# Four of a pass's sixteen GpSimd products by C moved to VectorE in a Mamba scan

## The reference

```
delta = softplus(xc @ xd_w @ dtp_w + dtp_b)
Bm, Cm = xc @ xB_w, xc @ xC_w
dA  = exp(delta[..., None] * A)                    # 512 channels x 16 states
dBx = (delta * xc)[..., None] * Bm[:, :, None, :]
h_t = dA_t * h_(t-1) + dBx_t                       # for each channel and state
y_t = sum over the 16 states of h_t * C_t;  y = y + D * xc
out = y * silu(z) @ out_w + res
```

## Time and profile before

| | us |
|---|---|
| median of 3 runs (lowest, highest) | 10204.22 (10203.43, 10209.12) |
| the profiled execution | 10211.62 |
| its span on the core | 10209.9 |

### The profile page before, as it was taken

How to read it: one execution, slowest core, us unless ns; L and a number is a source line. 1 busy time by engine, 2 the same in 40 slices (tenths; PEclk the granted TensorE clock), 3 DMA queues, 4 the chain that set the end, 5 groups by cost and what they waited for, 6 DMA issues and landing times. The chain is left out here.

```text
span 10209.9 us, 153036 instructions
## 1 busy us (share of the span) xinstructions
PE 8288.9 (81%) x42776; PEld 6783.2 (66%) x42776; DVE 8054.5 (79%) x10482; ACT 5907.1 (58%) x9202; POOL 7026.4 (69%) x7227
## 2 busy tenths in 40 slices
PE   5787878787878787878787878787878776999998
PEld 4666666666666666666666666666666664777776
DVE  4989898989898989898989898989898993333332
ACT  4656566666665666666666666666666662544443
POOL 4878788888888888888888888888888882000000
PEclk8888888888988888889898888888988887999998
DMA  2222222222222222222222222222222220000000
GB/s 92 99 90 94 100 94 98 95 99 94 97 97 91 94 96 96 98 96 94 89 89 86 94 94 100 94 99 93 100 94 100 94 84 24 11 12 8 12 10 9
DMA packets 414834, 818.78 MB, mean 80 GB/s; under 512 B 148918, under 2 KB 194138, under 8 KB 414042
## 3 DMA queue, kind: packets, MB, share of 16 engines
q1 hardware_dynamic: 410328, 806.69, 23.3%
q10 hardware_dynamic: 3714, 2.89, 0.1%
HBM read 783.16 MB, written 26.30 MB: 79 GB/s over the span
## 5 line engine op out<-in xcount | busy, mean ns | idle before, releaser
L781 ACT ACTIVATE decay<-delta,neg_a 128x512 f32<-128x512 f32 x4096 | 2799.4, 689 | 2378.0 <-DVE h_ps L982 1145.6
L543 POOL TENSOR_TENSOR bu<-b_all,u_buf 128x512 f32<-128x512 f32 x3072 | 3573.3, 1189 | 188.8 <-DVE h_ps L982 186.2
L982 DVE TENSOR_TENSOR_SCAN h_ps<-decay,bu 128x512 f32<-128x512 f32 x2304 | 2778.6, 1222 | 513.3 <-ACT decay L781 431.7
L1239 PE MATMUL y_ps<-ident,ch 128*128 128x128 f32 x16384 | 2504.0, 302 | 535.6 <-DVE ch L1002 412.8
L1239 PEld LDWEIGHTS y_ps<-ident,ch 128*128 128x128 f32 x16384 | 2132.8, 156 | 904.7 <-DVE ch L1002 552.4
L555 POOL TENSOR_TENSOR ch<-ch,c_all 128x512 f32<-128x512 f32 x1024 | 1326.3, 1295 | 966.9 <-DVE ch L982 779.1
L1002 DVE TENSOR_TENSOR ch<-h_ps,c_all 128x512 f32<-128x512 f32 x3072 | 1976.9, 671 | 0.0
L546 POOL TENSOR_TENSOR bu<-b_all,u_buf 128x514 f32<-128x514 f32 x1024 | 1244.8, 1236 | 12.7 <-DVE h_ps L982 9.1
L1123 PE MATMUL w_ps<-xn,in_w 128*128 128x257 f32 x4096 | 1095.1, 412 | 167.9 <-ACT xn L670 67.5
L986 DVE TENSOR_TENSOR_SCAN h_ps<-decay,bu 128x256 f32<-128x256 f32 x1536 | 1047.1, 737 | 59.2 <-POOL bu L546 33.9
L1123 PEld LDWEIGHTS w_ps<-xn,in_w 128*128 128x128 f32 x4096 | 806.9, 208 | 335.3 <-issue 75.7
(11 more groups left out here) (262 smaller groups left out, 11512.5 us busy)
## 6 DMA issues: line engine op xcount, KB each, us to landing
b_all<-bc_dram SPq DMA_DIRECT2D x512, 514.0 KB, 6.4
c_all<-bc_dram SPq DMA_DIRECT2D x512, 514.0 KB, 7.4
in_w<-in_L_attn_in_w SPq DMA_DIRECT2D x64, 1024.0 KB, 5.0
diag_store<-diag_dram SPq DMA_DIRECT2D x256, 256.0 KB, 3.7
x_in<-in_x SPq DMA_DIRECT2D x128, 256.0 KB, 3.6
out_w<-in_L_attn_out_w SPq DMA_DIRECT2D x64, 512.0 KB, 3.9
skip_diag<-skip_dram SPq DMA_DIRECT2D x64, 256.0 KB, 4.4
h_mid<-h_cur SPq DMA_DIRECT2D x32, 257.0 KB, 2.2
```

Source lines behind the costliest of these rows:

```text
L543: pool.tensor_tensor(bu[:, s % NBU, 0:NB * L].rearrange("p (b t) -> p b t", b=NB), b_all[:, n // NU, n % NU, :, 1:], u_buf[:, c % 2, :, 1: ...
L781: func(decay[:, s % NDP, :].rearrange("p (b t) -> p b t", b=NB), delta[:, c, :, 1:S], ACT.Exp, scale=neg_a[:, k, c, n:n + 1]).then_inc(dec ...
L982: dve.tensor_tensor_scan(h, decay[:, s % NDP, :], bu[:, s % NBU, 0:NB * L], 0.0, ALU.mult, ALU.add).then_inc(scan_done, 1)
L1239: last = pe.matmul(y_ps[:, k, :], ch[:, s % NPR, k * P:(k + 1) * P], ident[:, :], is_transpose=True, start=False, stop=(n == NST - 1 and k ...
```

## The change

`POOL_C` loses the states with n = 13 (s = 13, 29, 45, 61): GpSimd multiplies 12 states of a pass by C, VectorE 52 instead of 48. For the four states the scan writes into a PSUM slot in place of `ch`, VectorE's product follows that of state n = 12, and the counts that everyone waits for (`DVE_C`, `len(POOL_C)`) follow the list.

```diff
-POOL_C = range(1, STATES, 4)
+POOL_C = tuple(s for s in range(STATES) if s % 4 == 1 and s % NST != 13)
 DVE_C = STATES - len(POOL_C)
```

## The result

The change makes the kernel slower by 1%: 10306.29 us (median; 10297.58 to 10309.52) against 10206.67 us for the kernel before on the same chip, a ratio of 1.0098 [1.0086, 1.011], or +100 us where +49 was forecast. The direction and the engine were right, the size was not: the result lies above the range of 10215 to 10300 us. It is near the rival "Nothing hides" (10313 us) in size and shares half of its mechanism; the other half, waits for GpSimd's joint that come back, did not happen, so the nearness of the numbers is in part luck.

What follows compares the result with a forecast made beforehand. VectorE, 90% busy in the Mamba phase, was taken to set the pace. States 13, 29, 45 and 61 summed as 38 + 3 + 14 - 6 = +49 us, giving a median of 10253 us (+0.48%), range 10215 to 10300 us.

Steps and rivals of the forecast that it cites:

- Nothing hides: Rival, slower: TensorE's stretch after state 29 moves with VectorE, GpSimd joint waits come back; +109 us, 10313 us, chance 0.10.
- Who pays: VectorE sets the pace and pays 0.60 us per moved state, 154 us over 64 passes if nothing hides.
- GpSimd paces: Rival, faster: VectorE's stalls are due to GpSimd, so its relief of 5.2 us a pass gives -48 us; chance 0.04.
- Pinned SiLU: Rival: ScalarE's chain to the stall at scan 22 is not tied to scan 18, hiding state 13; +11 us, chance 0.10.
- State 13, +38: Before scan 22: ScalarE's chain moves with scan 18, so the stall keeps its length; 0.60 us every pass, 38 us.
- State 29, +3: Before `output` at scan 38: VectorE's wait for TensorE's gapless stretch hides the added 0.60 us; 3 us, bounds 0 and 38.
- thin place: Within state 29's cover: `y_t` comes about 0.6 us before TensorE wants it; charged 0.05 us, 3 us in all.
- State 45, +14: Scans 47 to 50: GpSimd's joint waits cover part, but decay 49 comes late; mean 0.22 us, 14 us.
- State 61, -6: At `step_size`: without GpSimd's product beside it, it saves 0.73 us against 0.60 us of cost; -6 us.
- Everything else at no cost: PSUM slots, counters, `ch` buffer waits, SyncE's reload and TensorE's earlier transposes were taken to cost nothing.

Runs made afterwards that it cites:

- the pair of edits: ScalarE's copies `xs_pad` and `y_t` both placed earlier: changed kernel +60.1 us against the kernel before (1.006); kernel before with both -11.3 us (0.9993).
- the fillers: Eight unused TensorE matmuls added before the projections: changed kernel +75.9 us against the kernel before (1.0074); kernel with only state 45 moved 10198.68 us (0.9998).

## Why the prediction was right or wrong, point by point

- **Who pays.** Right. VectorE pays for each added product, GpSimd's relief is worth next to nothing, and VectorE's busy time rose by 103 us (104 forecast). The rivals "GpSimd paces" and "Pinned SiLU" did not come true.
- **State 13, +38.** Paid, as forecast: +2.63 us a turn in the changed kernel, 42 us. That the sum comes so near is in part luck: it is 0.40 us in kinds 1 and 2 and 0.87 and 0.93 in kinds 3 and 4. "There is no GpSimd wait in between" was wrong: a short one before scan 16 hides 0.18 us in kinds 1 and 2, and the stall at 22 there is 1.42 instead of 1.62 us. Why kinds 3 and 4 pay more than 0.60 is not shown.
- **State 29, +3.** Wrong, and the largest miss on a single step. The step that failed is the overlap: the prediction took TensorE's stretch for its own work because its rows, of one turn, had no gap. The stretch is tied twice to VectorE's scans through ScalarE's queue. The prediction named one of the ties, `y_t` with 0.6 us of room, as the "thin place" and priced it at 3 us; in 34 of 45 passes there was no room, the stall at 38 stayed at 1.89 us, and the price is about 29 us, by the pair of edits. Of the rival "Nothing hides" this half was true.
- **State 45, +14.** The step itself was right, +0.90 us a turn (14 us): the joint's waits at 47 and 48 went, and decay 49 became late. The missing term is behind it. The prediction had TensorE's transposes start earlier "in front of nothing that VectorE waits for", at no cost; what came of it is TensorE's projections at the lower clock and the stall at `output`, 24 us by the fillers in the changed kernel, 42 in the kernel of state 45 alone. Both numbers include what fillers give in the kernel before, up to 8 us.
- **State 61, -6.** Right: the line's longest duration fell from 1410 to 695 ns, and the kernel with 61 alone is at -8.9 us.
- **Everything else at no cost.** Besides the clock, short pauses in VectorE's queue, at most 12 us.

The durations of `step_size`'s line (lowest/median/highest ns) after, against 659/684/1410 in the earlier trace rows:

```profile
L962 DVE SCALAR_TENSOR_TENSOR sp_l<-sp_l,diag_store x128: 659/674/695, 139.0 to 8477.4; 128x514 f32<-128x514 f32 x128
```

Together: 49 forecast, +26 for state 29, +16 to +24 for the clock (without or with what fillers give in the kernel before), and 0 to +12 for the pauses make 91 to 111 against 100. Each of the three is a difference of medians with an interval of some 10 us on either side, so the sum is closed no better than that. What stays open: what the pauses are, why an edit moves stalls in stretches that it doesn't touch, and why TensorE's clock falls with 45 alone by more than with all four.

## What to carry to other kernels

Before you call a stall a cover, follow its end back through every queue in order, a third engine's too: a copy that is ready may stand behind an operation that waits for the very engine whose delay you want to hide. Read more than one turn: a room of 0.6 us in one can be absent in most others. A merged row without a gap can still be slow by the clock, so look at the granted clock over just this row. And ask of a moved operation whether it shifts TensorE's work apart ahead of a dense stretch; the granted clock there belongs in the sum.

## What the runs showed of the hardware

- Work moved between two other engines changed TensorE's granted clock: the lower level went from 1.1 to 4.4 us a pass in one stretch of 10 us, and the same row of 16 records from 5.37 to 6.33 us; eight matmuls without use ahead of them gave a granted clock of 1.00, 3.68 us, and 42 us in all.
- VectorE paused for 0.37 us at places where nothing was late, and 4 or 12 fulfilled waits added to its queue removed one or both of the two pauses of a pass.
- A `scalar_tensor_tensor` with two SBUF inputs took 1.39 us beside GpSimd's product and 0.67 without it, while VectorE's product with one input in PSUM took 671 to 672 ns with GpSimd at 84% and at 79% of the phase.
